# Fifteen gathers of a tile in two parts: GpSimd issues eight, waits for the words of the next tile, and issues the other seven

## The reference, cut to what matters

```python
# x: (8, 2048, 256) float32, adj: (8, 2048, 2048) int32 of 0 and 1; W: (512, 256)
mask = adj != 0
scores = where(mask, -arange(N), -inf)
vals, idx = top_k(scores, 25)                 # the 25 neighbours with the lowest numbers
feats = x[idx], -inf where there is no neighbour
agg = feats.max(over the neighbours)
agg = where(degree <= 25, maximum(agg, 0), agg)
out = relu(concat([x, agg]) @ W + b)
result = layernorm(x + out)
```

## Time and profile before

| | |
|---|---|
| median of three runs | 3765.63 us (3760.57 to 3766.75) |
| the profiled execution | 3760.97 us |
| its span, first to last instruction | 3759.2 us |
| busy: PE, DVE, GpSimd, ACT | 64%, 62%, 55%, 34% |
| `numbered` (L467), first and last of 128 | 54.7 and 3712.8 us |
| gathers (L395) | 1920, and 30 more in three tiles with overflow |

### The profile page before, as it was taken

One profiled execution on the slowest core, in us unless ns is written; L12 is line 12 of the kernel. 1 busy time (PEld: TensorE's weight loads), 2 busy tenths in 40 slices (PEclk: granted clock), 3 DMA queues, 4 the chain that ended last, 5 costly groups with the idle time before them and its releaser, 6 DMA issues.

```text
span 3759.2 us, 47488 instructions
## 1 busy us (share of the span) xinstructions
PE 2407.7 (64%) x15529; PEld 1575.3 (42%) x15728; DVE 2335.7 (62%) x5090; ACT 1294.2 (34%) x2441; POOL 2077.1 (55%) x2078
## 2 busy tenths in 40 slices
PE   4664666664666766666766666646676766766664
PEld 2443434443444444444444444434444444444432
DVE  4665656655656656666656666656665766656665
ACT  4332333332333333333333333323333333333331
POOL 3554555554555555555555555555555555555554
PEclk8876777876778676777677777767766776677776
DMA  3554564555644565455555555555565555554554
GB/s 139 133 116 90 121 149 116 130 119 90 140 131 114 118 132 135 120 129 113 120 147 117 120 130 116 138 107 115 117 132 134 120 133 113 121 135 117 133 96 74
DMA packets 172601, 457.65 MB, mean 122 GB/s; under 512 B 42817, under 2 KB 92482, under 8 KB 154882
## 3 DMA queue, kind: packets, MB, share of 16 engines
q0 software_dynamic: 93600, 255.72, 38.4%
q1 hardware_dynamic: 78690, 198.31, 15.2%
HBM read 436.47 MB, written 16.78 MB: 121 GB/s over the span
## 4 chain that ended last, share of the span: by engine, by line
another core or an unknown queue 38%; DVE 21%; PE 18%; issue 11%; ACT 10%; POOL 2%; DMA 0%; DVEq 0%; POOLq 0%; ACTq 0%
PE near_ps L640 13%; DVE got L756 6%; ACT sign L428 5%; PE z_ps L615 2%; POOL got L395 2%; DVE key_left L791 1%; DVE word_top L793 1%; DVE word_top L788 1%; ACT numbered L467 1%; DVE got L850 1%; DVE got L856 1%; ACT limit L462 1%; DVE cand L768 1%; DVE top L802 1%
## 5 line engine op out<-in xcount | busy, mean ns | idle before, releaser
L395 POOL DMA_INDIRECT got<-in_x,index x1920 | 2035.5, 1060 | 1596.7 <-DVE index L773 910.1
L640 PE MATMUL near_ps<-parts,hot 128*128 128x256 bf16 x7152 | 1366.5, 358 | 675.7 <-issue 426.2
L640 PEld LDWEIGHTS near_ps<-parts,hot 128*128 128x128 bf16 x7152 | 865.9, 125 | 1126.1 <-issue 598.4
L756 DVE TENSOR_REDUCE got<-near_ps 128x256 f32<-128x2048 f32 (+6 forms) x376 | 692.0, 1840 | 441.0 <-remote 402.2
L467 ACT ACTIVATE numbered<-bits_ps 128x256 f32<-128x256 f32 x128 | 49.1, 384 | 1479.0 <-remote 1479.0
L783 DVE SCALAR_TENSOR_TENSOR key<-bits_ps,numbered 128x256 f32<-128x256 f32 x128 | 54.3, 424 | 722.2 <-ACT numbered L467 713.9
L660 PE MATMUL out_ps<-w_sb,h_t 128*128 128x256 f32 x1024 | 356.0, 508 | 0.0
L579 PE MATMUL z_ps<-mask_t,later_b 128*34 128x128 bf16 x2048 | 197.2, 272 | 219.5 <-ACT mask_t L432 183.3
L850 DVE TENSOR_TENSOR got<-got 128x2304 f32<-128x2304 f32 (+1 forms) x128 | 322.7, 2521 | 16.0 <-DMA got<-in_x,index 13.3
L457 ACT ACTIVATE val<-z_ps,rank_col 128x1024 int16<-128x1024 f32 x256 | 284.5, 1111 | 93.0 <-PE z_ps L615 72.9
L856 DVE TENSOR_TENSOR got<-got 128x1024 f32<-128x1024 f32 (+2 forms) x384 | 299.9, 781 | 13.2
(11 more groups left out here) (114 smaller groups left out, 1971.1 us busy)
## 6 DMA issues: line engine op xcount, KB each, us to landing
adj_sb<-in_adj_turned SPq DMA_DIRECT2D x128, 1024.0 KB
got<-in_x,index POOLq DMA_INDIRECT x1920
x_sb<-in_x SPq DMA_DIRECT2D x128, 128.0 KB
h_t<-in_x_turned SPq DMA_DIRECT2D x128, 128.0 KB
out<-result SPq DMA_DIRECT2D x128, 128.0 KB
heads<-in_x_near SPq DMA_DIRECT2D x8, 1536.0 KB, 10.8
w_sb<-in_L_gnn_W SPq DMA_DIRECT2D x1, 512.0 KB
hot<-vacant SPq DMA_DIRECT2D x32, 4.8 KB
```

Source lines behind the costliest of these rows:

```text
L395: pool.indirect_dma_start(out=to, out_offset=None, in_=x_rows, in_offset=bass.IndirectOffsetOnAxis(ap=at, axis=0)).then_inc(landed, 16)
L640: mm = pe.matmul(near_ps[:, s - k * ROUND:s - k * ROUND + 1, :], hot[:, a.i, s * P:(s + 1) * P], parts[:, (a.side * PARTS + n) * CH + c, N ...
L756: dve.tensor_reduce(got[:, a.i, FAR + k, :], near_ps[:, 0:n, :].rearrange("p q c -> p c q"), AX.X, ALU.max).then_inc(near_used, 1)
```

## The change

After the eighth gather of a tile (`s == FIRST_HALF`) GpSimd waits until `bits_ready` says that the words of the next tile are done, and adds one to `far_begun`, a semaphore that no engine waits for. Then it issues the other seven. Tile 127 has no next tile; for it PE adds one to `bits_ready` at the place where the words of tile 128 would stand.

```diff
@@ -26,6 +26,7 @@
 KEPT = 16
+FIRST_HALF = 8
 WORD = 8
@@ -402,6 +403,9 @@
                 pool.wait_ge(agg_ready, done(a.T - 2))
                 pool.sem_inc(far_begun, 1)
                 for s in range(FAR):
+                    if s == FIRST_HALF:
+                        pool.wait_ge(bits_ready, done(a.T + 1))
+                        pool.sem_inc(far_begun, 1)
                     gather(got[:, a.i, s, :], index[:, a.i, s:s + 1], gathered[a.i])
                 pool.wait_ge(flag_ready, done(a.T))
                 pool.sem_inc(flag_at_pool, 1)
@@ -683,6 +687,8 @@
                 a = Tile(g, side, t, 2)
                 if a.there:
                     words(a)
+                elif a.T == TILES:
+                    pe.sem_inc(bits_ready, 1)
                 a = Tile(g, side, t, 3)
                 if a.there:
                     rank(a, 1)
```

## The result

The changed kernel takes 4257.86 us (median of four runs, 4244.67 to 4269.64) against 3766.19 (also four) of the kernel before: 1.131 of it, with a 95% interval of 1.127 to 1.134. It is slower by 13%; the forecast was 4% faster. The profiled execution took 4269.64 us.

What follows compares the result with a forecast made beforehand. Bound: a 28.07 us loop per tile, words reported only after the last gather. New period 14.4 + 12.5 = 26.9; 1.17 us over 126 tiles saves 147, giving 3614 (3619 on the median's scale); likeliest 3450 to 3740, wider range 3430 to 3840.

Steps and rivals of the forecast that it cites:

- The loop of before: One tile, `numbered` to `numbered`: 4.80 + 0.84 + 20.00 + 2.43 = 28.07 us, through index, restart, gathers and late report.
- that the words are held while gathers are in hand: PE's words reach ScalarE only about 2.4 us behind the last gather, 9.7 us late in one tile.
- At best the 9.7 us delay is gone: After eight gathers, the next tile's words would be reported to ScalarE within 0 to 2.4 us.
- Last seven gathers, `combine` at b + 14.4: From b, when ScalarE has the words: 0.84 restart, 7.58 to seventh start, 5.7 landing, 0.3 for DVE.
- The rule weighed there: GpSimd DMA landing: about 2.0 us plus bytes by 436 GB/s, 2.3 us; would give period 23.5, 3185 us.
- From combine to the next words: Combine, reduce, cells, layer, words in unchanged order: 12.5 us, the middle of 11.2 and 13.7.
- The clock: PE's layer matmuls: 1.99 or 3.53 us by clock; 3.5 in every tile would mean the forecast is wrong.
- Two signs of being right: ScalarE's 1479 us before `numbered` under 700; a gap between eighth and ninth gather, none between fifteenth and next first.
- The late gathers cost more than the early index saves: At DVE's wait before `combine`, starting later than b + 15.6: slower, 3878 us middle, 4067 at the ends; chance 0.25.
- More than forecast: Landing 3.6 us and higher clock throughout: 12.0 + 11.2 = 23.2 us, 3160 us; period under 25.6, chance 0.12.
- The gathers don't hold the words: The words take 7 to 10 us by themselves: period 34 at least, 4500 us and more; chance 0.05.
- The rule set beside the rival: Skill advice to issue DMAs early and wait late; the change does the opposite for seven gathers per tile; no size.

Runs made afterwards that it cites:

- f3: Changed kernel with its wait behind the twelfth gather instead of the eighth, on a late chip: 3283 us, 0.875 of the kernel before.
- e7: Kernel before with empty slots spread over the graph's padding rows instead of all on one, on a prompt chip: 2843 us, 0.917 of before.
- e10: Changed kernel with empty slots spread over the graph's padding rows, on a prompt chip: 3308 us, 1.064 of the kernel before.
- series 12, 10, 8, 4: Changed kernel with its wait behind that many gathers, on prompt chips: 3092, 3299, 3724 and 4310 us; 1.003, 1.063, 1.197 and 1.388 of before.
- e8: Changed kernel, wait still behind the eighth gather but for the tile's own words, so already met, on a prompt chip: 3110 us, 1.002 of before.
- f2: Kernel before, each indirect gather fetching 64 bytes per partition instead of 1 KB, from fixed rows, on a late chip: 3745 us, 0.995 of before.
- e12: Kernel before with empty slots spread over the graph's padding rows, on a late chip: 3739 us, 1.003 of before.

## Why the prediction was wrong, point by point

**The loop of before** (28.07 us) and **that the words are held while gathers are in hand**: right for that chip; f3 shows it by moving the pause. "The mechanism behind that delay I don't know; the sum needs only that it ends with the gathers": there the fault begins. For the words it ends with them, but the counts and the near round that PE finishes meanwhile are held too, and the sum asked only about the words.

**"At best the 9.7 us delay is gone"**: gone it is, words to `numbered` 0.03 us.

**Last seven gathers, `combine` at b + 14.4**: right, 14.3 (and 14.8 on chip B). Landing was taken at 5.7. The rule weighed there, an estimate of 2.3 us by the Trainium skill ("DMA: Bandwidth & Descriptors", Anatomy of one DMA — SWDGE path), was set aside by the trace, and rightly for this kernel. The runs add why: the measured 5.7 belongs to one padding row; spread, the landing is 2.7 (e7), close to that estimate, and `combine` comes at 11.6 (e10).

**"From combine to the next words. The order of work is kept ... I take 12.5": this is the step that failed on that chip.** 17.8 us were measured. The order is kept, and that is what hurts: counts, flag and degree stand in PE's order ahead of the turn of `agg`, and with the pause moved they lie under the seven late and eight early gathers. The turn waits behind `agg` for 5.6 us in the tile shown and 4.4 in the median of all tiles (0.13 before the change, 0.06 on chip B). The other 1.0 of the excess of 5.3 us is the layer at the lower clock, 3.78 us where 12.5 stood for the middle of 1.99 and 3.53; the way from `combine` to the end of `agg` is 5.5 before and after. 14.3 + 17.8 = 32.1 us against 28.0 in 127 tiles makes 520 us; 492 were measured.

**The base, 28.07 us.** On prompt chips the forecast's parts hold: 14.8 and 12.8 measured for 14.4 and 12.5, period 27.5 for 26.9. What the sum is set against does not: 23.1 there and not 28.07, for `numbered` never waited for the gathers. There the seven late gathers move `combine` from 10.1 to 14.8 us behind `numbered`, 4.7 us, and the period grows by 4.4. That the loss has this cause is shown by the series 12, 10, 8, 4 at constant "back", and by e8.

**The clock**: the layer matmuls are at 3.78 us in the median after the change on both kinds of chip, the lower level, as was listed as a sign of being wrong. It is the smaller part, 1.0 us: on chip B "back" of 12.8 still lies between the 11.2 and 13.7 of the earlier trace rows.

**The other signs.** Two signs of being right came true on a slower kernel: the wait before `numbered` fell under 700 us (557.9), and the gap moved to between the eighth and the ninth gather. DVE's idle before L856 was 3.0 us per tile and not 4 to 6, for the reduce L762 ahead of it was late instead: its "remote" waits grew from 402 to 770 us, which was listed as a sign of being wrong.

**The rivals.** *The late gathers cost more than the early index saves* named this side, and in half a sentence ("the reduce ahead of `combine` is late too") the hold of other work; but its place was DVE's wait before `combine`, which came in time. Its 4067 us, and the range to 3840, left out the turn. (The 12.0 of *More than forecast* leaves out the 0.3 us of DVE; nothing hangs on that.) *The gathers don't hold the words* is refuted on late chips (f3) and true on prompt ones. The rule set beside the rival, to issue DMAs early and wait late (the Trainium skill, "DMA: Bandwidth & Descriptors", Rules for kernel authors), the series bears out on prompt chips: the more gathers late, the slower. On late chips it is not the whole: three late gathers there are 12.5% faster (f3).

**Open.** Why some chips report PE's work late while GpSimd issues indirect DMAs is not settled: not the bytes (f2), not the row (e12). Whether plain DMAs at full density would hold it was not seen on a late chip. Nor do the gathers in hand explain every report. In the tile shown the near matmuls of 2000.25 were reported around 2009.17, with eight more gathers running or to come, and the counts of 2004.45 not. Of the 120 late counts only 34 came behind the eighth and last gather of the row as in the tile shown; 59 came in the sixth or seventh, while GpSimd went on issuing. So that a hold ends with the gathers is shown for the words, and not for every report. The wait behind 12 with the padding spread, which might do most on a late chip, ran only on a prompt one.

## What to carry to other kernels

When a trace shows finished work that is reported late under some activity, moving one consumer out from under it is no gain in itself: list what else will then lie under it, and what stands behind that in each engine's order. Here the fifteen gathers stayed in one row, and the counts took the place of the words.

A price with an odd source (a landing of 5.7 us where other DMAs of the size take 2.3 to 2.9) is worth an experiment of its own: spreading the padding reads over fifteen rows gave 8.3% on a prompt chip, more than any placing of the wait.

Take the time of an unchanged kernel on more than one chip before a loop that rests on an unnamed wait is called its bound.

## What the hardware showed that was not expected

- The same program takes 3079 to 3109 us on four chips and 3730 to 3766 on two or three, with little spread on each. In the traces the difference is that PE's finished work is seen late while indirect gathers are issued: the words 8.7 us late in the median before the change (11.7 at most), the counts 12.1 after it (16.1 at most).
- Many reads of one HBM row are slow: a packet takes on average 0.46 us with one row, 0.24 with the kernel's own rows, 0.14 with the padding spread, at the same bytes.
- Fetching one sixteenth of the bytes with the same indirect DMAs changes the time by 0.5% on a late chip. GpSimd's pace stays at 1.25 us for each.
